# Second attention's opening in another order: x normalised ahead of the keys' low parts, half of its transposes between the key and the value products

## The reference

```python
q = (queries @ Wq).reshape(b, s, KV_HEADS, GROUP, HEAD_DIM)      # 8 x 4 x 16
k = (keys @ Wk).reshape(b, s, KV_HEADS, HEAD_DIM)                # 8 x 16 = 128 columns
v = (values @ Wv).reshape(b, s, KV_HEADS, HEAD_DIM)
scores = jnp.einsum('bqhgd,bkhd->bhgqk', q, k) * scale
attn = jax.nn.softmax(scores, axis=-1)
out = jnp.einsum('bhgqk,bkhd->bqhgd', attn, v)
return out.reshape(b, s, EMBED) @ Wo
```

## Time and profile before

| what | us |
|---|---|
| median of 3 runs | 1960.01 (1959.61 to 1960.69) |
| the profiled execution, its own time | 1959.41 |
| its span in the trace | 1957.7 |
| second attention: first key product | 981.60 |
| first transpose of x | 995.20 |
| first query product | 1014.00 |
| first score | 1037.96 |

### The profile page before, as it was taken

How to read it: one execution, slowest core, us unless ns; L and a number is a source line. 1 busy time by engine, 2 the same in 40 slices (tenths; PEclk the granted TensorE clock), 3 DMA queues, 4 the chain that set the end, 5 groups by cost and what they waited for, 6 DMA issues and landing times. The chain is left out here.

```text
span 1957.7 us, 28936 instructions
## 1 busy us (share of the span) xinstructions
PE 1832.3 (94%) x10418; PEld 1543.4 (79%) x10418; DVE 1379.4 (70%) x2796; ACT 611.0 (31%) x1712; POOL 604.2 (31%) x304
## 2 busy tenths in 40 slices
PE   7999999999999999996968979879889999999996
PEld 6888888888888888875855645666788888888885
DVE  5666666666666666676367855789788888888885
ACT  4321222221222212222025634531243333343330
POOL 6523333223333232303050005325334333243320
PEclk9999999999999999998989988989999999999998
DMA  4110111111111100102010003010101000010001
GB/s 166 59 37 20 43 50 47 50 47 50 47 50 47 42 28 26 50 14 81 0 43 1 1 11 97 22 39 22 44 22 44 33 32 32 32 43 32 32 12 55
DMA packets 29879, 78.43 MB, mean 40 GB/s; under 512 B 3857, under 2 KB 10705, under 8 KB 29425
## 3 DMA queue, kind: packets, MB, share of 16 engines
q1 hardware_dynamic: 29808, 77.50, 11.8%
HBM read 75.39 MB, written 2.10 MB: 40 GB/s over the span
## 5 line engine op out<-in xcount | busy, mean ns | idle before, releaser
L369 POOL TENSOR_TENSOR l0x_comb<-l0x_neg,l0x_bias 128x1024 f32<-128x1024 f32 x32 | 76.6, 2393 | 434.3 <-DVE l0x_probs L688 310.7
L609 ACT ACTIVATE l0x_probs_t<-bank 128x512 f32<-128x512 f32 x32 | 19.1, 597 | 546.2 <-PE bank L479 546.2
L2355 POOL TENSOR_TENSOR l3x_q<-l3x_q,l3x_cross 128x512 f32<-128x512 f32 x64 | 89.7, 1407 | 199.5 <-DVE l3x_q L1544 199.5
L38 PE MATMUL bank<-l0x_w_v_hi,ctx_lo 128*128 128x256 f32 x512 | 144.9, 283 | 0.0
L36 PE MATMUL bank<-l0x_w_v_hi,ctx_hi 128*128 128x256 f32 x512 | 144.9, 283 | 0.0
L37 PE MATMUL bank<-l0x_w_v_lo,ctx_hi 128*128 128x256 f32 x512 | 144.9, 283 | 0.0
L595 ACT ACTIVATE l0x_probs<-l0x_probs,l0x_top 128x129 f32<-128x129 f32 x256 | 99.4, 390 | 61.0 <-DVE l0x_top L692 61.0
L2486 ACT ACTIVATE l3x_probs<-l3x_probs,l3x_top 128x128 f32<-128x128 f32 x256 | 99.1, 389 | 37.4 <-DVE l3x_top L2555 37.3
L724 DVE TENSOR_TENSOR x<-x,bank 128x512 f32<-128x512 f32 x120 | 82.0, 683 | 38.7 <-PE bank L38 38.7
L361 POOL TENSOR_TENSOR l0x_w_qk_lo<-l0x_raw_qk,l0x_w_qk_hi 128x1024 fp32r<-128x1024 f32 x31 | 75.1, 2423 | 110.0 <-ACT l0x_w_qk_hi L602 110.0
L36 PE MATMUL bank<-l3x_qin_hi,l3x_w_q_hi 128*128 128x512 f32 x256 | 105.9, 414 | 3.1 <-PEq L119 3.1
(11 more groups left out here) (464 smaller groups left out, 5250.3 us busy)
## 6 DMA issues: line engine op xcount, KB each, us to landing
l0x_raw_qk<-L_qk_dram SPq DMA_DIRECT2D x31, 512.0 KB, 4.3
l0x_raw_v<-L_v_dram SPq DMA_DIRECT2D x16, 512.0 KB, 5.5
l0x_raw_o<-L_o_dram SPq DMA_DIRECT2D x16, 512.0 KB, 5.4
l3x_raw<-L_q_dram SPq DMA_DIRECT2D x16, 512.0 KB, 3.5
l3x_raw<-L_o_dram SPq DMA_DIRECT2D x16, 512.0 KB, 3.5
kv_raw<-L_kv_dram SPq DMA_DIRECT2D x8, 512.0 KB, 3.5
l0x_ctx_raw<-ctx_t_dram SPq DMA_DIRECT2D x4, 512.0 KB, 5.8
x<-x_dram SPq DMA_DIRECT2D x8, 256.0 KB, 8.1
```

What stands on the lines that cost most here:

```text
L38: return pe.matmul(out, lhs[1], rhs[0], start=False, stop=stop)
L369: pool.tensor_tensor(comb[:, :, :], neg[:, :, :], bias[:, j:j + 1, :].to_broadcast([P, B, P]), ALU.add).then_inc(comb_ready, 1)
L609: act.activation(probs_t[:, 0:BH, :], bank[6][:, :].rearrange("p (b n) -> p b n", b=BH), ACT.Copy).then_inc(t_act, 1)
L2355: pool.tensor_tensor(dst[:, part], dst[:, part], cross[n][:, :], ALU.add).then_inc(rotated, 1)
```

## The change

On PE the key products come first, then the transposes of batches 0 to 3, then the value products, then the transposes of batches 4 and 5 (behind `kt_done`) and 6 and 7 (behind `vt_done`). On ACT the high parts of `xt` for batches 0 to 3 stand between the keys' and the values' evictions, those for 4 to 7 behind the values', and the output weights' high part between the two halves of `q`. On DVE the scaling of x stands ahead of the keys' low parts. POOL's and SP's lists are unchanged, and no instruction is added or taken away.

```diff
--- before.py
+++ after.py
@@ -1167,23 +1167,31 @@
             @block.tensor
             def _(pe):
 
-                pe.wait_ge(core.l1_kv_split, 1)
-                for n, done in enumerate((kt_full, vt_full)):
+                def from_context(n, done):
                     for half in range(2):
                         for c in range(DC):
                             mm = product(pe, bank[2 * n + half][:, :], [w_kv[s][:, c, n * P:(n + 1) * P] for s in range(2)],
                                          [core.cin[s][:, c, half_of(half)] for s in range(2)], c == 0, c == DC - 1)
                         mm.then_inc(done, 1)
-                for b in range(B):
+
+                def transpose_x(b):
                     pe.wait_ge(core.xn_done, B * n_norm + b + 1)
-                    if b == BH:
-                        pe.wait_ge(kt_done, 2)
-                    if b == BH + 2:
-                        pe.wait_ge(vt_done, 2)
                     for c in range(DC):
                         mm = pe.transpose(bank[xt_bank(b)][:, c * P:(c + 1) * P], xn[:, b, c * P:(c + 1) * P],
                                           core.ident[:, :])
                     mm.then_inc(core.xt_full, 1)
+
+                pe.wait_ge(core.l1_kv_split, 1)
+                from_context(0, kt_full)
+                for b in range(BH):
+                    transpose_x(b)
+                from_context(1, vt_full)
+                pe.wait_ge(kt_done, 2)
+                transpose_x(BH)
+                transpose_x(BH + 1)
+                pe.wait_ge(vt_done, 2)
+                transpose_x(BH + 2)
+                transpose_x(BH + 3)
                 pe.wait_ge(w_ready, 1)
                 for half in range(2):
                     pe.wait_ge(core.xt_copied, B * n_norm + (half + 1) * BH)
@@ -1286,16 +1294,22 @@
                 for half in range(2):
                     act.wait_ge(kt_full, half + 1)
                     act.activation(kt[0][:, half_of(half)], bank[half][:, :], ACT.Copy).then_inc(kt_hi, 1)
+                def x_high(b):
+                    act.wait_ge(core.xt_full, B * n_norm + b + 1)
+                    act.activation(xt[0][:, :, b * P:(b + 1) * P],
+                                   bank[xt_bank(b)][:, :].rearrange("p (c t) -> p c t", c=DC), ACT.Copy).then_inc(xt_hi, 1)
+
+                for b in range(BH):
+                    x_high(b)
                 for half in range(2):
                     act.wait_ge(vt_full, half + 1)
                     act.activation(vt[:, half_of(half)], bank[2 + half][:, :], ACT.Copy).then_inc(vt_done, 1)
-                for b in range(B):
-                    act.wait_ge(core.xt_full, B * n_norm + b + 1)
-                    act.activation(xt[0][:, :, b * P:(b + 1) * P],
-                                   bank[xt_bank(b)][:, :].rearrange("p (c t) -> p c t", c=DC), ACT.Copy).then_inc(xt_hi, 1)
-                act.wait_ge(raw_loaded, 32)
-                act.activation(w_o[0][:, :, :], raw[:, :, :], ACT.Copy).then_inc(w_hi, 1)
+                for b in range(BH, B):
+                    x_high(b)
                 for half in range(2):
+                    if half == 1:
+                        act.wait_ge(raw_loaded, 32)
+                        act.activation(w_o[0][:, :, :], raw[:, :, :], ACT.Copy).then_inc(w_hi, 1)
                     for g in range(G):
                         act.wait_ge(q_full, half * G + g + 1)
                         act.activation(q[0][:, g, half_of(half)], q_bank(half, g)[:, :], ACT.Copy, scale=SCALE
@@ -1339,14 +1353,14 @@
                     dve.bn_aggr(core.mv[:, b, :], core.stats[:, b, :]).then_inc(core.mv_done, 1)
                 dve.wait_ge(core.mv_done, B * (n_norm + 1))
                 dve.tensor_scalar_add(core.var_eps[:, :], core.mv[:, :, 1], EPS).then_inc(core.var_done, 1)
+                dve.wait_ge(core.rstd_done, n_norm + 1)
+                for b in range(B):
+                    dve.tensor_scalar(xn[:, b, :], core.x[:, b, :], core.mv[:, b, 0:1], core.rstd[:, b:b + 1],
+                                      ALU.subtract, ALU.mult).then_inc(core.xn_done, 1)
                 for half in range(2):
                     dve.wait_ge(kt_hi, half + 1)
                     dve.tensor_tensor(kt[1][:, half_of(half)], bank[half][:, :], as_f32(kt[0][:, half_of(half)]),
                                       ALU.subtract).then_inc(kt_done, 1)
-                dve.wait_ge(core.rstd_done, n_norm + 1)
-                for b in range(B):
-                    dve.tensor_scalar(xn[:, b, :], core.x[:, b, :], core.mv[:, b, 0:1], core.rstd[:, b:b + 1],
-                                      ALU.subtract, ALU.mult).then_inc(core.xn_done, 1)
                 for b in range(B):
                     dve.wait_ge(xt_hi, b + 1)
                     dve.tensor_tensor(xt[1][:, :, b * P:(b + 1) * P],
```

## The result

The changed kernel takes 1942.38 us (median of 4 runs, 1940.92 to 1944.37) against 1959.81 (4 runs): a ratio of 0.9911, 95% interval 0.9894 to 0.9929. The profiled execution took 1940.92 us, its span is 1939.2. The forecast was 1942.5.

A forecast was written before the change was run, and what follows sets the result against it. PE bounds the kernel (busy 1832.3 of 1957.7 us), save a 21.3 us hole while POOL holds DVE's scalings. Replacing it with 3.8 us of transposes gains 17.5: 1960.01 - 17.5 = 1942.5 us, range 1940.8 to 1946.0.

The forecast's parts named there:

- The cause: DVE's eight scalings of x take 21.3 us because DVE gets one in between two of POOL's instructions.
- Scaling at 0.457 us: Moved ahead on DVE, eight scalings start at 984.2 at a pitch of 0.457 us and end at 987.9.
- over 0.6 us ahead of POOL: Scalings end at 987.9, 0.6 us before POOL's subtraction for the query weights starts at 988.52.
- meeting of a scaling with POOL: Rival: POOL starts before the scalings end, holding one at most 4.6 us; time 1943.4, chance 0.05.
- The hole of 21.3 us replaced by transposes: PE's hole before the query products becomes 32 transposes of 0.12, 3.8 us; first query product 17.5 us earlier.
- the floor of the forecast: PE's work alone in the opening: no more than 17.7 us can come from there.
- DVE's subtractions beside POOL's `kd`: `xt` and `q` subtractions beside `kd` cost nothing extra; rival that POOL holds them: 1952.3, chance 0.04.
- `kd` and the output weights as later partners: Score inputs arrive in time, `kd` with slack 10.6 us; rival that a late partner takes the gain: 1960, chance 0.02.
- The clock: Rival: PE's clock falls at the sixteen-transpose groups, 3.1 us, 1945.6, chance 0.08; staying down: 1969.4, chance 0.02.

The follow-up runs named there:

- four scalings late: Changed kernel with the scalings of batches 4 to 7 put back behind the keys' low parts on DVE: 1960.62 us, run once more 1957.33 us.
- scaling's order alone: Kernel before with only DVE's part of the change, the scaling of x ahead of the keys' low parts: 1941.94 us, ratio 0.9904.
- POOL waits: Kernel before with one wait more: POOL starts the query weights' low part only when all eight scalings are done: 1945.57 us, ratio 0.9930.
- scaling on ACT: Kernel before with the scaling of x made by ACT behind the keys' copies, DVE making only a bias: 1946.92 us, ratio 0.9935.
- scores early: Changed kernel with the first two score units put between the groups of the second half of the query products: 1937.46 us, ratio 0.9890.
- PE and ACT alone: Changed kernel with DVE's two loops put back in the old order: 1962.41 us, ratio 1.0016.

## Why the prediction was right

The time was 1942.38 against 1942.5, inside the range of 1940.8 to 1946.0. The mechanism is the one that was forecast; that the point is hit to 0.1 us is in part luck, since stretches without an edit move by more than that from trace to trace (table above), and the opening by itself gained 17.96 us and not 17.5. By its steps:

- **The cause** stood in the row of the scalings, 3814 ns where 541 was their price, and in POOL's timeline beside it. Two experiments confirm it from different sides: POOL's work taken away (3.73 us for eight) and the scaling taken off DVE. One detail of the reading was off: the first scaling sat out two instructions of POOL, the subtraction and the fill, so that five scalings were held behind six instructions, and the last three were free.
- **Scaling at 0.457 us**, over 0.6 us ahead of POOL: 3.74 us for eight. They ended at 985.92 + 3.74 = 989.66, and POOL's subtraction started at 990.06. The gap was 0.4 us, less than forecast, and nothing met. So the changed kernel has no meeting of a scaling with POOL, and four scalings late has four. The Trainium skill (SBUF — State Buffer, section "SBUF: two separate sides") states that the loser blocks fully, for the whole of the other's instruction. The trace of before agrees: up to 4975 ns for a scaling.
- **The hole of 21.3 us replaced by transposes.** I counted 1.9 us for each sixteen, from the merged row, which runs to the last one's end. What they hold PE up for is from the first start to the next product's start: 997.75 - 996.05 = 1.70. For two groups that is most of the 0.46 us by which the opening came out shorter than forecast (17.96 against 17.5), and it is why the floor of the forecast, no more than 17.7 us, didn't hold.
- **DVE's subtractions beside POOL's `kd`**: taken at nothing on the row of `kt_lo`, and so it is: 0.62 us each beside POOL, 0.61 with POOL idle (4.87 for eight).
- **`kd` and the output weights as later partners**: `kd` ended at 1007.08 + 3.60 = 1010.68, 11.0 us ahead of the first score; the output weights' low part ended at 1016.27, in time. Neither absorbed the gain.
- **The clock** stayed at 1.00 through both groups of transposes. It did fall later, at the start of the scores, which I had not forecast; from the first score to the start of the second transposes of probabilities it is 1029.88 - 1021.71 = 8.17 us, against 8.07 before, since that stretch goes by DVE.

What the prediction missed was where the gain came from. It priced the change as one path, on which scaling, transposes and evictions all moved, and didn't ask what each part was worth without the others. DVE's two swapped loops give all that the medians show, and PE's reorder without them costs 1.6 us of opening. The numbers for this stood in the text: with all transposes behind the values PE comes to the same sum of work, and the evictions fit in.

## What to carry to other kernels

When an instruction that scales from SBUF to SBUF on DVE is several times as long in one place as the same form elsewhere, look at POOL's timeline beside it before looking at what it waits for: the profile shows the hold as busy time. Put such instructions into POOL's idle time, or give them to ACT. DVE's subtractions that read PSUM weren't held here, but a scaling that reads PSUM wasn't run. When one engine is starved by another, try the supplier's order first: reordering the starved engine alone put independent work behind the late one and made it slower.

## What the runs showed of the hardware

The first scaling of before, by itself:

```profile
990.17 4.97 DVE L1348 TENSOR_SCALAR l1x_xn<-x,mv,rstd 128x512 f32<-128x512 f32 x1
```

- The hold is paid by both. POOL's `kd` took 3.77 or 3.78 us where a scaling had got in just ahead of it, and 3.59 to 3.63 us in every run without that (changed kernel, scaling's order alone, POOL waits, scaling on ACT, scores early): about 0.18 us for each scaling that got in. In four scalings late the last `kd` has one ahead of it and none behind, and takes 3.78.
- POOL's fill of `v`, which reads nothing, held a scaling as well. The scaling in the line above lasted to 995.14, past the subtraction's end at 993.12 and the fill's at 994.86. None got in between the subtraction and the fill, while one got in ahead of every `kd`; in four scalings late the first late scaling (994.37, 4.99 us) comes out only behind the fill, too. Why isn't shown.
- ACT's scalings (0.72 us) and DVE's subtractions out of PSUM (0.62 us) were not held by the same POOL instructions.
- With no edit there, the granted clock fell to 0.58 over 3.4 us at the start of the scores in the changed kernel's trace, and stayed at 1.00 in before's. An idle stretch of PE of 2.0 us stands there in both. It fell there in the changed kernel's second trace (0.58), the scaling's order alone (0.52), PE and ACT alone (0.64) and POOL waits (0.71) too, and stayed at 1.00 in both traces of four scalings late and in scaling on ACT, each time behind the same idle stretch. So the idle stretch alone doesn't decide it; what does isn't shown.
